# Half a line of padding: all five products of the last stage with the loaded operand on 0 and the streamed one on 64 modulo 128 bytes

## What is computed

```python
z = rmsnorm(u, pre_norm_w) @ in_proj_w.T            # then a 3-tap convolution, split into x2, x1, v
y = (yconv + xv * D_skip) * x2                      # long convolution of xv = x1 * v
y = y @ out_proj_w.T + u                            # "out"
zm = rmsnorm(y, post_norm_w)
mlp = gelu(zm @ l1_w.T) * (zm @ l2_w.T) @ l3_w.T    # "mlp" (l1, l2), then "down" (l3)
x = x + layernorm(y + mlp)
h = gelu(layernorm(x) @ (W1 + scale * m1).T + b1)   # "up"
x = x + layernorm(h @ (W2 + scale * m2).T + b2)     # "w2"
```

## The kernel before

| product | function, line | loaded | streamed | written | matmuls a step |
|---|---|---|---|---|---|
| mlp | `mlp_block` 1569 | `wl1`, `wl2`, `wrest` | `mt` | `ps_ring` | 66 |
| up | `ffn_up` 1621 | `we1` | `xt` | `ps_ring` | 48 |
| out | `out_projection` 1589 | `yt` | `wout` | `ps_o` | 12 |
| down | `mlp_down` 1606 | `pt`, `pstack` | `wl3`, `wstack` | `ps_m` | 32 |
| w2, two halves | `ffn_down` 1635 | `ht` | `we2` | `ps_w` | 24 + 24 |
| turns, two | `transpose_unit` 1563 | `rows` | `ident` | `ps_rt` | 4 + 4 |

## Time and profile before

### The profile page before, as it was taken

One profiled execution on the slowest core, in us unless ns is written; L12 is line 12 of the kernel. 1 busy time (PEld: TensorE's weight loads), 2 busy tenths in 40 slices (PEclk: granted clock), 3 DMA queues, 4 the chain that ended last, 5 costly groups with the idle time before them and its releaser, 6 DMA issues.

```text
span 1075.0 us, 24951 instructions
## 1 busy us (share of the span) xinstructions
PE 1050.8 (98%) x9012; PEld 1008.5 (94%) x9012; DVE 877.8 (82%) x2322; ACT 710.8 (66%) x1589; POOL 299.5 (28%) x575
## 2 busy tenths in 40 slices
PE   8899999999999999999999999999999999999998
PEld 7777888899989999999999999989999999999997
DVE  7999998774788888888887878897888888887776
ACT  7879887764456666666666666656666666666644
POOL 7677775470101112111111111111112111111111
PEclk9999999999999999999999999999999999999999
DMA  3337977986322222233222222432222223222000
GB/s 130 120 117 236 294 216 196 363 318 151 83 66 41 54 57 50 52 52 58 59 60 58 52 51 60 122 96 41 60 51 50 52 53 59 59 58 60 21 21 31
DMA packets 112491, 102.83 MB, mean 96 GB/s; under 512 B 7552, under 2 KB 103744, under 8 KB 112112
## 3 DMA queue, kind: packets, MB, share of 16 engines
q1 hardware_dynamic: 111136, 98.67, 36.2%
q0 software_dynamic: 736, 2.51, 0.6%
q10 hardware_dynamic: 496, 0.05, 0.0%
HBM read 75.75 MB, written 30.70 MB: 99 GB/s over the span
## 4 chain that ended last, share of the span: by engine, by line
PE 67%; DVE 6%; issue 2%; ACT 1%; POOL 0%; POOLq 0%; DVEq 0%; ACTq 0%
PE ps_ring L1551 35%; PE ps_w L1551 16%; PE ps_m L1551 9%; PE ps_o L1551 4%; PE ps_rt L1566 2%; DVE base L1373 1%; PE ps_w L1561 1%; DVE bn L1277 1%; PE ps_m L1617 1%; DVE prod L1320 0%; DVE ht_l L1289 0%; DVE pt_l L1289 0%; POOL sc L1129 0%; ACT rows L1254 0%; DVE yrow L1512 0%
## 5 line engine op out<-in xcount | busy, mean ns | idle before, releaser
L1129 POOL TENSOR_TENSOR sc<-sc,small 128x2 f32<-128x2 f32 x127 | 94.5, 744 | 676.8 <-DVE sc L1501 404.6
L1194 ACT ACTIVATE gate<-ps_ring 128x256 f32<-128x256 f32 x192 | 73.0, 381 | 129.7 <-PE ps_ring L1551 128.9
L1215 ACT ACTIVATE hid<-ps_ring,small 128x256 f32<-128x256 f32 x256 | 112.1, 483 | 24.2 <-PE ps_w L1551 13.4
L1551 PE MATMUL ps_ring<-mt_l,wl_h 128*128 128x256 f32 x640 | 125.5, 277 | 2.6 <-DVE mt_l L1289 2.6
L1551 PE MATMUL ps_ring<-mt_h,wl_h 128*128 128x256 f32 x640 | 125.5, 277 | 1.8 <-DVE prod L1320 1.3
L1551 PE MATMUL ps_ring<-mt_h,wl_l 128*128 128x256 f32 x640 | 124.9, 277 | 0.0
L1289 DVE TENSOR_TENSOR ht_l<-hid,ht_h 128x256 fp32r<-128x256 f32 x256 | 103.1, 423 | 16.5 <-ACT ht_h L1219 10.6
L1551 PE MATMUL ps_ring<-xt_h,we_h 128*128 128x256 f32 x512 | 104.8, 285 | 2.5 <-DVE prod L1320 2.4
L1551 PE MATMUL ps_ring<-xt_h,we_l 128*128 128x256 f32 x512 | 101.3, 279 | 0.0
L1551 PE MATMUL ps_ring<-xt_l,we_h 128*128 128x256 f32 x512 | 101.3, 279 | 0.0
L1320 DVE TENSOR_TENSOR prod<-ps_ring,gate 128x256 f32<-128x256 f32 x192 | 80.7, 420 | 24.2 <-ACT gate L1194 20.6
(11 more groups left out here) (203 smaller groups left out, 2720.2 us busy)
## 6 DMA issues: line engine op xcount, KB each, us to landing
toep_scratch<-taps_scratch SPq DMA_DIRECT2D x26, 512.0 KB, 7.4
toep<-toep_scratch SPq DMA_DIRECT2D x26, 512.0 KB, 8.8
xa<-in_x SPq DMA_DIRECT2D x16, 512.0 KB, 4.9
x_scratch<-x2c SPq DMA_DIRECT2D x16, 512.0 KB, 3.7
x2s<-x_scratch SPq DMA_DIRECT2D x32, 256.0 KB, 6.7
xa_c<-in_x SPq DMA_DIRECT2D x32, 256.0 KB, 2.7
xb_c<-in_x SPq DMA_DIRECT2D x32, 256.0 KB, 2.7
yin<-seq SPq DMA_DIRECT2D x124, 64.0 KB, 5.5
```

Of the source, the lines that this page charges most:

```text
L1129: nc.gpsimd.tensor_tensor(sc[:, to], sc[:, to], neg_half[:, 0, 0:CC], ALU.pow).then_inc(S[done], 1)
L1194: nc.scalar.activation(gate[rows_of, m % 2], ring[m % RING][rows_of, 0], ACT.Gelu_apprx_tanh).then_inc(S["gate_done"], 1)
L1215: nc.scalar.activation(hid[:, m % HIDS], block_of, ACT.Gelu, bias=b1s[:, m:m + 1]).then_inc(S["hid_done"], 1)
L1551: mm = nc.tensor.matmul(out, lhs(a, kk), rhs(b, kk), start=(j == 0), stop=(closed and j == len(todo) - 1))
```

## The change

One tensor of 64 bytes (`HALF_LINE`, 16 floats) is put wherever the next group of tensors shall start on the other half of a 128-byte line, and some tensors are put elsewhere in the list. No instruction is added, taken out or moved on any engine, and no wait is changed: rows of both programs are the same from the first to the last on all five. What changes are addresses.

```diff
+        def half_line(ctx, name):
+            sb(ctx, name, [P, HALF_LINE])
...
         ident = sb(whole, "ident", [P, P])
+        half_line(whole, "streamed0")
         small = sb(whole, "small", [P, SMALL])
...
         seq = sb(whole, "seq", [P, P, KB, COLS])
         wout = [sb(whole, f"wout_{s}", [P, KB, D], F32R) for s in "hl"]
+        wl3 = [sb(whole, f"wl3_{s}", [P, FULL, D], F32R) for s in "hl"]
+        wstack = sb(whole, "wstack", [3 * REST, D], F32R)
+        half_line(whole, "loaded0")
         wl1 = [sb(whole, f"wl1_{s}", [P, KB, FULL * P], F32R) for s in "hl"]
         wl2 = [sb(whole, f"wl2_{s}", [P, KB, FULL * P], F32R) for s in "hl"]
         wrest = [sb(whole, f"wrest_{s}", [P, KB, 2 * REST], F32R) for s in "hl"]
-        wl3 = [sb(whole, f"wl3_{s}", [P, FULL, D], F32R) for s in "hl"]
-        wstack = sb(whole, "wstack", [3 * REST, D], F32R)
...
-        we1_high, we2_high = (sb(ctx, name, shape, F32R) for name, shape in
-                              (("we1_h", [P, KB, H]), ("we2_h", [P, HB, D])))
+        we1_high = sb(ctx, "we1_h", [P, KB, H], F32R)
+        half_line(ctx, "streamed1")
+        we2_high = sb(ctx, "we2_h", [P, HB, D], F32R)
+        half_line(ctx, "loaded1")
         with ExitStack() as weights_made:
             base1 = sb(weights_made, "base1", [P, KB, H])
+            half_line(weights_made, "streamed2")
             base2 = sb(weights_made, "base2", [P, HB, D])
         we1 = [we1_high, sb(ctx, "we1_l", [P, KB, H], F32R)]
+        half_line(ctx, "streamed3")
         we2 = [we2_high, sb(ctx, "we2_l", [P, HB, D], F32R)]
-        sb(ctx, "offset", [P, OFFSET])
...
-        yt = [sb(ctx, f"yt_{s}", [P, KB, TC], F32R) for s in "hl"]
...
+        half_line(ctx, "loaded2")
+        yt = [sb(ctx, f"yt_{s}", [P, KB, TC], F32R) for s in "hl"]
         pt = [sb(ctx, f"pt_{s}", [P, FULL, TC], F32R) for s in "hl"]
```

More of the change, by code:

```diff
@@ L37 @@
 SMALL = 32
+HALF_LINE = 16
 FIRST = GROUPS // 2
@@ L955, in phase_c @@
     RING = 4
-    OFFSET = 16
     FIRST_OUT = (14, 5, 3)
@@ L963, in phase_c @@
     with ExitStack() as ctx:
-        we1_high, we2_high = (sb(ctx, name, shape, F32R) for name, shape in
-                              (("we1_h", [P, KB, H]), ("we2_h", [P, HB, D])))
+        half_line = v["half_line"]
+        we1_high = sb(ctx, "we1_h", [P, KB, H], F32R)
+        half_line(ctx, "streamed1")
+        we2_high = sb(ctx, "we2_h", [P, HB, D], F32R)
+        half_line(ctx, "loaded1")
         with ExitStack() as weights_made:
             base1 = sb(weights_made, "base1", [P, KB, H])
+            half_line(weights_made, "streamed2")
             base2 = sb(weights_made, "base2", [P, HB, D])
         we1 = [we1_high, sb(ctx, "we1_l", [P, KB, H], F32R)]
+        half_line(ctx, "streamed3")
         we2 = [we2_high, sb(ctx, "we2_l", [P, HB, D], F32R)]
         b2s = sb(ctx, "b2s", [P, D])
-        sb(ctx, "offset", [P, OFFSET])
         xa = sb(ctx, "xa_c", [P, CC, D])
```

## The result

The changed kernel takes 1083.06 us (median of 4 runs, 1082.57 to 1083.60) against 1076.68 for the kernel before on the same chip: ratio 1.0051, with a 95% interval of 1.0034 to 1.0069. The medians differ by 6.4 us, where 16.9 had been forecast (1093.6 us). The profiled execution took 1083.53 us, with a span of 1081.8.

The account below looks back on a forecast made before the run. TensorE's matmul spacing was taken to bound 669 of 1075 us. +0.58 us a step over 27.3 steps gives +15.8, plus 1.2 outside: 1093.75 us against the profiled execution, 1093.6 against the median; range 1075 to 1097.

Parts of the forecast that it names:

- mlp, up, turns:* same places: Last stage: the change leaves the operand places of mlp, up and turns as they were; up forecast +0.00 us a step.
- the first observation: From the timeline before: behind a turn, a product at 0 / 64 comes out long (up, 27 of 32) and stays long.
- out and down on up's places: Out and down, now at up's half, carry on its long spacing of 117.7 ns: +0.03 and +0.12 us a step.
- w2's first half, +0.08: First 24 matmuls of w2: the long spacing goes on from up through out and down, 2.82 us, +0.08 a step.
- w2's second half, +0.06: 24 matmuls behind the second turn, now at 0 / 64 like up, so long with start-up: 2.91 us, +0.06 a step.
- mlp, +0.29: 66 matmuls behind w2: mlp follows a long 0 / 64 product and does not recover, 7.77 us, +0.29 a step.
- Outside of the stretches, +1.2: Out, down and w2 of the first steps and last two: some 250 short matmuls turn long, +1.2 us in total.
- Partly long: Rival: `pstack` or the second turn resets the rhythm, so only part turns long; 1083 or 1089 us, chance 0.20.
- Nothing moves: Rival: something other than halves sets each product's rhythm, so the time stays 1076.7 +/- 1 us; chance 0.13.
- the rule: Skill page: TensorE's two independent SBUF read ports make weight loads free, so places could matter to nothing, 1076.7 us; trace doesn't settle it.
- Faster: Rival: up comes out of the turn short and the short rhythm is never lost; -8.5 us, 1068 us, chance 0.19.
- theory 4: From the follow-up runs: a product's rhythm is set by its places paired with those of what ran just before, turns included.

Follow-up runs that it names:

- w2 mended: The changed kernel with `we2` on 64 modulo 256 for both halves, so all of w2 is at distance 192: 1076.67 us, ratio 0.9989 to the kernel before.
- the series above: Kernel without the computation: copies input to output, then runs series of 48 matmuls on all 16 pairs of places modulo 256; the same work takes 5.70 to 6.00 us.

## Why the prediction was wrong

**What bounds the kernel** was right: no idle time on TensorE in 669 us before and after, and the change acts through the spacing alone. So was the form of the sum, steps of 24.5 us times 27.3. **The two rhythms** of 113.3 and 117.7 ns, and that they persist, were right.

**The step that failed** is "*mlp, up, turns:* same places", and with it the first observation, "Behind a turn, 0 / 64 comes out long". The prediction expected up to come out long as now, and let its rhythm go on through out, down and w2. Places modulo 128 are not the ones that count: modulo 256 up moved from 0 / 64 to 128 / 64 in two of three passes, and that alone makes it short (5.54 us with `we1_h` alone moved). That is 0.21 us a step of the missing 0.36; the other part is out and down, forecast +0.15 and measured -0.02, since there was no long rhythm to go on. The observation is false on its own ground too: with mlp ahead of it at distance 0, the same up on 0 / 64 behind the same turn is short. Its 27 cases of 32 were one case, seen 27 times, of a loop in its steady state.

**out and down on up's places: the rhythm goes on.** Right as a rule, with the opposite rhythm: up short, out short.

**w2's first half, +0.08,** measured +0.10, for another reason than the one given. down ahead of it is short; the `pstack` matmul lies between, and behind it all three passes come out long (0.95, 0.94 and 0.95 us for eight), the middle one at distance 192 with the two at 64. With w2 mended it is 2.74. The prediction had `pstack` as the place of a rival that would *end* a long rhythm; here a long one begins there.

**w2's second half, +0.06,** measured +0.04. Its first pass takes 1.03 us, as before: before, gaps of up to 127 ns behind the turn fell to 113 within the pass, now they are 117 to 120 from the second on. The pass at distance 192 goes over to short within four matmuls (0.91), and the last, at 64, is long from its first gap on (0.95).

**mlp, +0.29,** measured +0.30. That mlp inherits from w2 was the mechanism, and where places do not change between the two the runs show it: long behind a long w2, short behind a short one, within one kernel (all six at 192). On the places that the prediction had in mind, mlp on 0 / 64, a long w2 ahead gives the 7.77 that it forecast (unit matrix moved). But in the changed kernel mlp's places had changed as well, against what the text said, and w2's last pass, at 64, is not on them. That mlp inherits there too is argued; another kernel has mlp at 192 long behind a short w2 (up and mlp on 0 / 192).

**Outside of the stretches, +1.2:** 6.4 - 6.0 leaves 0.4. `phase_b`, put at 0: the last stage's first out begins at 249.49 in place of 249.35, so it was 0 within 0.2 us; and the first whole step begins at 351.88 in both kernels, so nothing was lost ahead of it. DVE's tensors: 534.6 / 27.0 steps = 19.8 us a step, as 539.1 / 27.3 = 19.8 before. Nothing there.

**The rivals.** *Partly long* gave 1083 for one case, and 1083 was measured, but by another way: it had w2's second half and mlp unchanged and all else long. Here it is almost the reverse. *Nothing moves* falls, and with it what the prediction had made of the rule. Moving operands by 64 or 128 bytes against each other moved the time from 1072.4 to 1088.7 us with the same instructions. The Trainium skill (SBUF — State Buffer, section "Who interferes with whom") says that TensorE's two read ports are independent and that only the pair shared by DVE and GpSimd causes contention; no other engine worked in the series above, yet 120.0 ns at distance 0 stand against 113.3 in five of the series at 192. Here the measurement decides. *Faster* named the right first event, an up that comes out of the turn short and hands that on. Its price for up, -0.21, is what was measured; it failed at w2, where distance 64 begins.

**What stays open.** Which of the two rhythms a product takes behind a turn. It depends on the turn's own places and on what ran before the turn, and it repeats, every step or every two or three; in which way, the runs don't say, and theory 4, which took only the last operation ahead, missed one of its four runs. Nor is it shown why 0 / 64 keeps what 64 / 0 hands on while 0 / 192 turns it over. Buffers of other engines that alternate from step to step are a rival that no run tests: `yrow` has two slots, and the two-step pattern keeps to them in both sequences. The three-step pattern does not keep to the three slots of `x1`: its short mlp falls on chunks 4 to 16 in the first sequence and on 20 to 29 in the second, every third, and those are other slots. The loads look alike in both rhythms: each starts about 3 ns behind the start of the matmul ahead, and it is the way from there to its own matmul that takes 110 ns in the short rhythm and 115 in the long one, in mlp and up of one step of the kernel before. That it is reads of loaded and streamed rows that meet in SBUF is argued from the role of the distance, not shown.

## What to carry to other kernels

Where TensorE has no idle time and weights are loaded for every matmul, look at the spacing of the matmuls by product, and at the starts of both operands modulo 256 bytes: not equal, 96 or 128 apart (120.0, 120.0 and 118.7 ns for 256 columns). Neighbouring products on one and the same pair take over each other's rhythm, the long one as well as the short: the three kernels with all six on one pair took 1075.6, 1080.2 and 1088.7 us. Between the two rhythms of 64 and 192, 113.3 and 117.8 ns, places alone don't choose; try two or three layouts and measure, since 64 bytes under a tensor elsewhere can cost 0.8%. And a pattern that a loop repeats 27 times is one observation: before it is made a rule, find it behind another run-in.

## What the hardware showed that was not expected

- The distance of the two operands' starts modulo 256 bytes sets the least gap of back-to-back matmuls with their own loads: 120.0 ns at 0, about 118.7 at 128 (24 of 24 series). In the series at 128 the gaps are uneven, 115 to 122 ns, once they have settled; at 64 and 192 they are even to 2 ns.
- At 64 and 192 there are two stable gaps, 113.3 and 117.8 ns. A product keeps one through 66 matmuls, and the next product with the same places takes it over; where places change, one can go over into the other within four matmuls.
- The state survives a turn of four transposes and gives patterns that repeat every one, two or three steps: 24.31 and 24.68 us by turns in one kernel, 24.55, 25.03 and 25.15 in another.
- Moving the unit matrix by 64 bytes cost 0.35 us a step in products that never read it.
